# Cross-attention and feed-forward on one core: value rows staged in another place, and their stores issued ahead of their loads

## What is computed

```python
def xattn(xn, ctx, Wq, Wk, Wv, Wout, bout):     # xn = layernorm(x); 8 heads of 128
    qh, kh, vh = heads(xn @ Wq), heads(ctx @ Wk), heads(ctx @ Wv)
    sim = qh @ kh.T * 128 ** -0.5
    mean = sim.mean(-1)
    attn = softmax((sim - mean) * 1.5 + mean)   # over all 154 context rows
    return merge(attn @ vh) @ Wout + bout

def ffn(x, W_r, W_k, W_v, mu_r, mu_k):          # x = layernorm of the sum so far
    xr, xk = mix(mu_r, x, x_prev), mix(mu_k, x, x_prev)    # x_prev: the row before, per batch
    return sigmoid(xr @ W_r.T) * (relu(xk @ W_k.T) ** 2 @ W_v.T)

x = x + xattn(layernorm(x), ctx, ...)
x = x + ffn(layernorm(x), ...)
```

## Time and profile before

| | us |
|---|---|
| runs: median, lowest, highest | 798.74, 797.66, 798.83 |
| profiled execution | 798.89 |
| its span | 797.1 |
| TensorE busy (matmuls) | 754.3 |
| VectorE busy | 519.3 |
| ScalarE busy | 434.4 |
| GpSimd busy | 127.0 |
| mean granted TensorE clock | 0.972 |

### The profile page before, as it was taken

The page is one execution under the profiler, slowest core; times in us unless marked ns, Lnnn a source line. Parts: engine busy times, 40 slices in busy tenths (PEclk is TensorE's granted clock), DMA queues, the critical chain, the costliest instruction groups (busy, mean ns, idle before and its releaser), DMA issues.

```text
span 797.1 us, 13508 instructions
## 1 busy us (share of the span) xinstructions
PE 754.3 (95%) x3918; PEld 659.7 (83%) x3918; DVE 519.3 (65%) x1078; ACT 434.4 (54%) x1211; POOL 127.0 (16%) x277
## 2 busy tenths in 40 slices
PE   7984876999999999999999999999999999999977
PEld 6954765889888898989888988889898989898866
DVE  2661776676767666666777676766666677766561
ACT  2661754756656574646465664656564646555322
POOL 1100210111020212121211102021212121110211
PEclk9997798999999999999999999999999999999999
DMA  9857415444454445444443444344544444343310
GB/s 308 315 149 200 117 63 154 127 144 149 136 155 123 139 128 164 135 155 138 132 147 113 153 135 151 116 137 138 164 132 158 138 123 148 117 144 97 103 54 26
DMA packets 87584, 112.16 MB, mean 141 GB/s; under 512 B 10152, under 2 KB 61634, under 8 KB 87556
## 3 DMA queue, kind: packets, MB, share of 16 engines
q1 hardware_dynamic: 87555, 111.82, 45.2%
HBM read 61.55 MB, written 50.23 MB: 140 GB/s over the span
## 4 chain that ended last, share of the span: by engine, by line
PE 83%; DVE 6%; ACT 3%; DMA 3%; issue 2%; SPq 2%; POOL 1%; POOLq 0%; DVEq 0%; ACTq 0%
PE ffn L489 11%; PE ffn L491 11%; PE ffn L490 11%; PE scores L490 8%; PE scores L491 8%; PE attended L489 8%; PE attended L491 8%; PE attended L490 8%; PE scores L489 8%; DMA value_rows<-staged 2%; PE scores L615 1%; PE attended L527 1%; PE attended L526 1%; ACT probs L720 1%; DMA handed<-x_rows 1%
## 5 line engine op out<-in xcount | busy, mean ns | idle before, releaser
L489 PE MATMUL scores<-A_hi,xT_hi 128*128 128x462 f32 (+1 forms) x384 | 136.1, 354 | 6.3 <-DVE xT_lo L914 5.1
L490 PE MATMUL scores<-A_lo,xT_hi 128*128 128x462 f32 (+1 forms) x384 | 136.2, 355 | 0.0
L491 PE MATMUL scores<-A_hi,xT_lo 128*128 128x462 f32 (+1 forms) x384 | 135.6, 353 | 0.0
L489 PE MATMUL attended<-B_hi,pT_hi 128*128 128x512 f32 x288 | 113.4, 394 | 7.6 <-DVE pT_lo L914 7.1
L720 ACT ACTIVATE probs<-scores,neg_max 128x154 f32<-128x154 f32 x256 | 96.4, 387 | 39.4 <-DVE neg_max L969 38.8
L491 PE MATMUL attended<-B_hi,pT_lo 128*128 128x512 f32 x288 | 113.4, 394 | 0.0
L490 PE MATMUL attended<-B_lo,pT_hi 128*128 128x512 f32 x288 | 113.3, 393 | 0.0
L969 DVE TENSOR_REDUCE neg_max<-scores 128x3 f32<-128x462 f32 (+1 forms) x96 | 55.4, 583 | 81.9 <-PE scores L491 81.9
L1219 POOL TENSOR_SCALAR var<-stats 128x1 f32<-128x1 f32 x64 | 12.2, 191 | 467.6 <-DVE stats L920 466.5
L489 PEld LDWEIGHTS scores<-A_hi,xT_hi 128*128 128x128 f32 x384 | 73.5, 191 | 14.2 <-DVE xT_lo L914 6.1
L490 PEld LDWEIGHTS scores<-A_lo,xT_hi 128*128 128x128 f32 x384 | 73.4, 191 | 6.0
(11 more groups left out here) (160 smaller groups left out, 1593.7 us busy)
## 6 DMA issues: line engine op xcount, KB each, us to landing
prob_rows<-probs SPq DMA_DIRECT2D x32, 704.0 KB, 3.4
probs_handed<-prob_rows SPq DMA_DIRECT2D x128, 176.0 KB, 3.3
x_rows<-normed SPq DMA_DIRECT2D x62, 256.0 KB, 2.1
handed<-x_rows SPq DMA_DIRECT2D x248, 64.0 KB, 1.9
x_in<-in_x SPq DMA_DIRECT2D x32, 256.0 KB, 3.5
out<-x SPq DMA_DIRECT2D x32, 256.0 KB, 2.2
value_rows<-staged SPq DMA_DIRECT2D x8, 308.0 KB
B_rows<-value_rows SPq DMA_DIRECT2D x4, 576.0 KB
```

What stands on the lines that cost most here:

```text
L489: te.matmul(psum, left[0], right[0], start=first, stop=False)
L490: te.matmul(psum, left[0], right[1], start=False, stop=False)
L491: return te.matmul(psum, left[1], right[0], start=False, stop=last)
```

## The change

The staging buffers 0 to 3 move from W_k's turned copy to the start of the region `at_B` (16 KB per partition, over the keys, the context and Wk, where `B_hi` will lie later); buffers 4 to 7 stay over W_r's turned copy. `x_early` moves behind them in the same region. On SyncE stores 0 to 5 go out one behind the other, then `hand_probs(0)`, stores 6 and 7, the bias, and then the four loads; `store_x(3)` comes behind all loads, where it stood ahead of the last one. On ScalarE the wait for the stores of buffers 0 to 3 is dropped, and the wait for buffers 4 to 7 moves down to W_r's copies (`weights_hi(4..7)`). The stores of buffers 0 to 3 are covered for `B_hi` by the wait for the loads.

```diff
--- before.py
+++ after.py
@@ -172,7 +172,6 @@
         ctx1 = sb("ctx1", [J - P, C], at=at)
         at += size_of([P, C])
         wk = sb("wk", [P, CC, inner], at=at)
-        x_early = sb("x_early", [P, D], at=at)
         at += size_of([P, CC, inner])
         wv = sb("wv", [P, CC, inner], at=at)
         assert at + size_of([P, CC, inner]) <= at_ffn_weights
@@ -180,7 +179,10 @@
         vT_hi = sb("vT_hi", [P, HEADS, J], F32R, at=at_pT)
         vT_lo = sb("vT_lo", [P, HEADS, J], F32R, at=at_pT_rows)
 
-        staged = [sb(f"staged{h}", [P, 2, D], at=at_ffn_weights + h * size_of([P, 2, D])) for h in range(HEADS)]
+        staged = [sb(f"staged{h}", [P, 2, D], at=(at_B if h < HEADS // 2 else at_ffn_weights) + h * size_of([P, 2, D]))
+                  for h in range(HEADS)]
+        x_early = sb("x_early", [P, D], at=at_B + HEADS // 2 * size_of([P, 2, D]))
+        assert HEADS // 2 * size_of([P, 2, D]) + size_of([P, D]) <= size_of([P, FULL, D])
 
         wout = sb("wout", [P, HEADS, D], at=at_mix)
         wout_lo = sb("wout_lo", [P, HEADS, D], F32R, at=at_mix)
@@ -449,17 +451,13 @@
             hand_x(2)
             sp.wait_ge(consts_ready, 1)
             store_probs(0)
-            store_values((0, 1, 2))
+            store_values(range(0, 6))
+            hand_probs(0)
+            store_values((6, 7))
             load_bias()
-            hand_probs(0)
-            load_values(0)
-            store_values((3, 4))
-            load_values(1)
-            store_values((5, 6))
-            load_values(2)
-            store_values((7,))
+            for q in range(4):
+                load_values(q)
             store_x(3)
-            load_values(3)
             hand_x(3)
             store_probs(1)
             hand_probs(1)
@@ -860,8 +858,6 @@
             pack_hi(0)
             x_norm(3, 3)
             values_even()
-            for i in range(4):
-                act_e.wait_ge(B_stored[i], 32)
             for n in range(0, 4):
                 weights_hi(n)
             for b in range(3):
@@ -872,6 +868,8 @@
             for i in range(3):
                 probs_hi(0, i)
             pack_hi(1)
+            for i in range(2, 4):
+                act_e.wait_ge(B_stored[i], 32)
             for n in range(4, 8):
                 weights_hi(n)
             x_norm(4, None)
```

## The result

The change makes the kernel faster. The four runs of the changed kernel have a median of 788.99 us (788.06 to 791.97), the kernel before 798.2 us beside them: a ratio of 0.9891, 95% interval 0.987 to 0.9913. By that ratio the gain is 8.7 us, within 6.9 to 10.4 (the two medians alone differ by 9.2). The profiled execution of the changed kernel took 788.43 us, its span is 786.6 us, 10.5 us shorter than before.

What follows compares the result with a forecast made beforehand. TensorE bounds the body, which starts late because SyncE's queue order makes ScalarE wait 18.6 us. A gain of 14.6 less 2.4 for late transfers, 12.2 us, gives 786.6 us; range 783.5 to 791.0, 8 times in 10.

Steps and rivals of the forecast that it cites:

- rival B: Four loads in flight run slower than 178 GB/s; ending at 80 to 82, the gain is 9.2 to 7.2 us; 13%.
- Part (1): W_k's turned copies on ScalarE no longer wait for stores; the chain behind tile 1's exponentials moves 14.6 us earlier.
- Part (2): W_r's copies on ScalarE now wait for stores 4 to 7, reached at about 74.4; it costs nothing.
- Part (3): Issues on SyncE: hand_probs(0) at 57.1, stores 6 and 7 and bias rows by 60.7, the four loads by 68.1.
- Part (4): The four bunched loads follow hand_probs(0) and stores 6 and 7, move at 206 GB/s and end at 77.0.
- Part (5): Behind the loads, store_x(3) lands at 78.2, then hand_x(3) and store_probs(1) follow; exponentials(2, 0) is 2.4 us late.
- A: No transfer is late: small ones pass, or loads overlap at 250 GB/s or more; 784.1 us; 20%.
- C: TensorE's granted clock: 1.2 GHz lasts 4 us longer under tile 3's scores; 787.5 to 788.7 us; 7%.
- D: No gain: the stall changes place, ScalarE stops at W_r's copies or values_hi(0) until about 91; 2%.
- E: Slower: bunched loads crawl, store_x(3) and store_probs(1) land behind them; about 801.5 us at 100 GB/s; 2%.
- One for one: Behind attend(2) TensorE sets the pace, so an earlier start there is an equally earlier end of the kernel.

Runs made afterwards that it cites:

- e3: The changed kernel with the store of tile 3's normalised rows issued ahead of the first store of the value rows: 788.17 us, ratio 0.9878.
- e2: The kernel before with SyncE's new order of issues alone, staging buffers and ScalarE's wait as before: 789.94 us, ratio 0.9893.
- e7: The changed kernel with the store of tile 3's rows issued from ScalarE's queue behind the exponentials of tile 1: 787.34 us, ratio 0.9871.
- e6: e3 with each store of 77 partitions cut into one of 64 and one of 13: 787.36 us, ratio 0.9863.
- e5: e3 with each quarter's large load cut into three, pieces alternating between quarters 0 and 2, then 1 and 3: 785.13 us, ratio 0.9831.
- e10: As e5, but the pieces alternate between quarters 0 and 1, then between 2 and 3: 788.26 us, ratio 0.9864.

## Why the prediction was right, and where it was off

The forecast was 786.6 us, the measurement 788.99, inside the range of 783.5 to 791.0; the gain forecast was 12.2 us and 8.7 (6.9 to 10.4) came. The forecast's own range, 785.5 to 788, misses it. The wide range held because it took in rival B, whose condition (loads that end at 80 to 82) is what happened.

- *Part (1), 14.6 us.* Right. The exponentials of tile 1 end at 69.21 (forecast 69.45), W_r's copies start at 74.04 (74.4). (The rows give 0.30 and not 0.31 for the last matmul of the scores, which changes nothing.)
- *Part (2), W_r's wait costs nothing.* Right, no wait stands before them.
- *Part (3), the issues.* Off by 2.2 us: the two bias rows took 2.59 us to issue and not 0.9, and `hand_probs(0)` 2.53 and not 1.75. One of the two bias issues took 2.26 us. In e3 the two took 0.62 together, but the four small transfers of the first load 2.67, where those of the third took 1.43; why single issues stretch here was not tried. The loads were issued from 62.90 to 70.31, not from 60.7 to 68.1.
- *Part (4), the loads end at 77.0.* This is the term that was mis-sized. The last load lands at 80.88, 3.9 us later, and even the slow bound (178 GB/s, near 79) was too early. The store lands 0.3 us behind it and not 1.3, so what hangs on the store is 2.9 us late (81.14 against 78.2). The bytes give most of it. From 58 to 81 the DMA engines moved 208 GB/s, which is 4.78 MB, where the sum had 1.35 + 2.85 + 0.26 = 4.46. The sum starts at 58.0 with `hand_probs(0)` and leaves out store 5, though part (3) has it go out at 56.7: 0.32 MB, an estimated 1.6 us at 206 GB/s. (The trace records the landing of stores 4 and 5 at 61.44.) The rate gives some 0.8 us more: 190, 217 and 179 GB/s from 66 to 78, 195 in the mean and not 206, make 14.6 us of 2.85 MB in place of 13.8. The rest lies in the end, where the rate falls to 157 from 78 to 80 and then to nothing. That split is an estimate from the rows, not tried. The late issues of part (3) are not the cause by what the runs show. The first load is issued 3.4 us after the last staging copy began in e2 and e7, 4.5 in the change, 5.4 in e6, and the last load lands 23.9, 23.7, 22.5 and 23.3 us after it: earlier issues came with no earlier landing.
- *Part (5).* Right in mechanism and order, late by the error of part (4): `x_norm(4)` waits 5.2 us, and `exponentials(2, 0)` starts at 86.56, put down to `store_probs(1)`, and not at 83.4. From the landing it is 5.4 us to there, forecast 5.2. But in e3 taking it away brings only 0.9 us, not 2.4 (28.14 less 27.25 us, from the last staging copy): the loads themselves are late, and the text counted them as just in time for `values_hi(0)` at 77.2.
- *The rivals.* With the last load at 80.9 the outcome is B's by its condition, and B had 13% where the forecast had 56%. B's numbers for 80 (`exponentials(2, 0)` at 86.4, a gain of 9.2) are close to those measured, though 788.99 lies in the gap between the forecast's own range and B's (789.5 to 791.5). B's sign, a wait for the value rows at `values_hi(0)`, did not show, because the store landed just behind them and `x_norm(4)` stands ahead. It shows in e3. A is out: the store landed last. Its argument, 279 GB/s of stores alone, is not quite what the earlier trace rows show: by the landing records of the kernel before, load 1 ends at 69.74, inside that stretch. C's sign came, at no price that shows: the granted clock is 0.66 from 96 to 100 and 0.50 from 100 to 104, so the scores of tile 3, from 98.7 on, ran at the lower level for over 5 us, where it was some 3.4 before. But from `exponentials(2, 0)` to `attend(2)` it is 41.3 us here and 41.5 before. D and E did not come near.
- *One for one.* Nearly: `attend(2)` came 9.1 us earlier (0.4 of it a shorter start-up, by the last staging copy), and the span is 10.5 us shorter. Of the 1.4 us between them about 1.0 is the clock, by an estimate from the rows below. In both kernels TensorE idles for over 6 us before `attend(2)` and begins it at 1.2 GHz. The kernel before, from 137 to 150, where 2.4 GHz comes back:

```profile
137.00:142.00 5.00, 4.98 (x12) 3.93 (x13) 2.92 (x7) 2.03 (x9) 1.00 (x3) 0.50 0.98 232
142.00:150.00 8.00, 8.00 (x40) 6.71 (x39) 6.66 (x18) 6.24 (x22) 0.89 (x2) 0.97 0.18 57
```

At 0.50 for 5 us and 0.97 for 8, the lower level lasts some 5.5 us from there. In the changed kernel's stretches it is 0.58 from 128 to 132, so some 3.5 us, and 2.0 us at half speed less are 1.0.

What stays open: whether a store in ScalarE's queue can pass loads issued before it (e7 does not test it), why the same loads land 22.5 to 23.9 us after the last staging copy in kernels that issue them alike, why the clock came back sooner, and why e2's last store landed so late.

## What to carry to other kernels

When a wait is removed from a chain, list every transfer behind it and when it would arrive if it started at its earliest: here two different edits, each alone, took away the same wait or most of it and met nearly the same arrival of bytes. Add up all bytes that are in flight at the start of the backlog, the last transfer issued before it too. A small transfer issued behind bulk loads landed with them here (10.8 us in place of 2.1), so issue it first if its data is there. That took its wait away, and the gain of 0.8 us is within the noise. Where loads go into 32 partitions each, try alternating between the halves of the partitions; here that brought the loads 2.1 to 2.9 us earlier.

## What the runs showed of the hardware that was not expected

- Two streams of loads into 32 partitions each, 64 partitions apart, moved 245 GB/s in a stretch of 14 us where streams 32 apart moved 224 (e5, e10, one profiled execution each, other transfers included).
- The issues of the two bias rows took SyncE 2.59 us together in the changed kernel, behind eight stores and a hand-over, and 0.90 in the kernel before, behind three stores. One of the two took 2.26 us.
- A store of 256 KB from ScalarE's queue took 9.2 us with three loads issued ahead of it from SyncE's queue, where such a store takes 2.1 us in the median.
